# A slot table of 128 partition rows, and source lanes stored as bytes, in a fused graph network

## The reference

```python
h = relu(layernorm(x))
for W, b in lift:                                 # 8 times
    g = l2_normalize(segment_sum(h[src] * edge_weight[:, None], dst))
    h = l2_normalize(concatenate([h, g]) @ W + b)
for W, b in proj:                                 # 4 times
    g = segment_sum(h[src] * edge_weight[:, None], dst)
    h = tanh(concatenate([h, g]) @ W + b)
x = x + h
```

## Time and profile before

| | |
|---|---|
| median of 3 runs | 12909.68 us |
| profiled execution | 12883.4 us, its span 12881.8 us |
| busy in the span: PE, DVE, ACT, POOL | 7922.8, 9363.2, 3162.7, 4996.6 us |
| mean DMA rate | 94 GB/s |
| granted clock of TensorE, mean | 0.765 |

### The profile page before, as it was taken

How to read it: one execution, slowest core, us unless ns; L and a number is a source line. 1 busy time by engine, 2 the same in 40 slices (tenths; PEclk the granted TensorE clock), 3 DMA queues, 4 the chain that set the end, 5 groups by cost and what they waited for, 6 DMA issues and landing times.

```text
span 12881.8 us, 342702 instructions
## 1 busy us (share of the span) xinstructions
PE 7922.8 (62%) x130026; PEld 5298.1 (41%) x130039; DVE 9363.2 (73%) x19419; ACT 3162.7 (25%) x7975; POOL 4996.6 (39%) x5027
## 2 busy tenths in 40 slices
PE   2444444410376777776776777777667777777773
PEld 1333333300365666665665666666522222222221
DVE  7666666637665675666666666666699999999995
ACT  0000000008421212212211212212134444444431
POOL 2666666620112112111111111111077777777771
PEclk9999999995678787787787787787755565555555
DMA  4000000017645454454454454454422212222221
GB/s 152 21 21 21 21 20 21 21 69 285 203 136 149 134 153 136 132 168 120 132 166 119 135 161 132 139 161 135 116 43 36 35 35 35 35 35 35 35 34 17
DMA packets 717799, 1210.29 MB, mean 94 GB/s; under 512 B 176136, under 2 KB 338731, under 8 KB 713491
## 3 DMA queue, kind: packets, MB, share of 16 engines
q1 hardware_dynamic: 433940, 1057.96, 25.5%
q0 software_dynamic: 146832, 68.64, 5.9%
q10 hardware_dynamic: 136012, 67.95, 2.1%
HBM read 1051.25 MB, written 140.48 MB: 93 GB/s over the span
## 4 chain that ended last, share of the span: by engine, by line
PE 29%; DVE 21%; issue 16%; another core or an unknown queue 7%; DMA 3%; POOL 2%; DVEq 1%; ACT 1%; SPq 0%; POOLq 0%; ACTq 0%
PE psum L1927 10%; PE psum L1959 8%; PE psum L1942 6%; DVE space L1439 3%; DVE space L1472 2%; DVE space L1473 2%; PE psum L2034 2%; DMA space<-src_rows 2%; DVE space L1435 2%; DVE space L1407 1%; PE psum L2004 1%; DVE space L1417 1%; DVE space L1484 1%; DVE space L1477 1%
## 5 line engine op out<-in xcount | busy, mean ns | idle before, releaser
L787 POOL DMA_INDIRECT space<-feature_table,space x2000 | 2422.1, 1211 | 615.2 <-issue 614.9
L714 POOL TENSOR_TENSOR claim_out<-claim_in 128x1 f32<-128x1 f32 x443 | 94.8, 214 | 6431.4 <-DMA table<-space 2772.0
L1138 DVE TENSOR_TENSOR space<-psum,space 128x320 f32<-128x320 f32 x2400 | 1065.8, 485 | 1769.1 <-PE psum L1942 1740.1
L1622 ACT ACTIVATE space<-psum 128x375 f32<-128x375 f32 x2400 | 952.4, 435 | 3886.4 <-PE psum L1927 2877.6
L2050 PE MATMUL psum<-w_mix,space 64*128 64x448 f32 x4144 | 1842.3, 986 | 0.0
L1959 PE MATMUL psum<-space 128*128 128x96 bf16 x24000 | 1472.1, 214 | 472.3 <-issue 410.8
L723 POOL DMA_INDIRECT slots<-space x1568 | 1510.5, 963 | 449.3 <-issue 413.8
L1927 PE MATMUL psum<-space 128*32 128x125 fp8e4 x72000 | 1483.7, 230 | 310.0 <-issue 304.1
L1959 PEld LDWEIGHTS psum<-space 128*128 128x128 fp8e4 x24000 | 1199.3, 101 | 716.8 <-issue 608.4
L1927 PEld LDWEIGHTS psum<-space 128*32 128x32 bf16 x72000 | 1165.2, 101 | 619.7 <-issue 613.1
L1942 PE MATMUL psum<-identity,space 128*128 128x128 f32 x6000 | 964.7, 296 | 359.5 <-ACT space L1622 346.6
(11 more groups left out here) (278 smaller groups left out, 12198.9 us busy)
## 6 DMA issues: line engine op xcount, KB each, us to landing
space<-marks SPq DMA_DIRECT2D x2400, 320.0 KB
space<-src_rows SPq DMA_DIRECT2D x102, 640.0 KB, 4.7
marks<-space SPq DMA_DIRECT2D x100, 640.0 KB, 3.1
space<-distances ACTq DMA_DIRECT2D x200, 320.0 KB
space<-block_ids SPq DMA_DIRECT2D x198, 200.0 KB
slots<-space SPq DMA_DIRECT2D x82, 448.0 KB, 9.2
space<-feature_table,space POOLq DMA_INDIRECT x2072
slots<-space POOLq DMA_INDIRECT x1608, 2.1
```

The lines of the kernel that those rows point to most:

```text
L787: g.indirect_dma_start(out=gathered_rows[0:SLOTS, half, t, :], out_offset=None, in_=feature_table, in_offset=bass.IndirectOffsetOnAxis(ap= ...
L1138: v.tensor_tensor(row[:, half, :], slots_of_unit[:, half, :], slot_w[:, bass.ds(at * UNIT_TILES + k * HALF_TILES, HALF_TILES)].rearrange(" ...
L1622: a.activation(to[:, s0:s1, :, :], pair_picked[:, bank, 0:(s1 - s0) * PICK_COLS].rearrange("p (k c r) -> p k c r", k=s1 - s0, r=CAP), ACT.Copy
```

## The change

The table's first dimension becomes 128 (`LANES`) instead of 125 (`SLOTS`). The three new rows are never scattered to and hold the empty records of the fill. The loads of the pieces and of the records, and DVE's copies, take all 128 partitions. The list and the spill records move back by 6000 records, and the number of fills stays 82 (663,696 records before and 669,696 now, in steps of 8192). POOL still gathers 125 rows per tile, and the steps from slot to slot in the scattered addresses are unchanged.

The source lanes are stored as bytes (U8): in the turned copy, in `src_rows` and in the ring that is compared. The value for "no lane" becomes 200 instead of -1, since a byte can't be negative. On every engine the instructions and their order stay the same.

```diff
@@ constants
+    U8 = mybir.dt.uint8
-    LIST_ROW = SLOTS * SLOT_TILES
+    LIST_ROW = LANES * SLOT_TILES
+    NO_LANE = 200.0
@@ tensors
-    src_rows = nc.dram_tensor("src_rows", [SRC_CHUNKS * LANES, LANES], BF16).ap()
+    src_rows = nc.dram_tensor("src_rows", [SRC_CHUNKS * LANES, LANES], U8).ap()
-    slot_tiles = slots[0:LIST_ROW, :].rearrange("(p t) w -> p t w", p=SLOTS)
+    slot_tiles = slots[0:LIST_ROW, :].rearrange("(p t) w -> p t w", p=LANES)
-        source_ring = ring_flat[:, 0:UNIT_COLS].bitcast(BF16).rearrange("p (s c) -> p s c", s=2)
+        source_ring = ring_flat[:, 0:UNIT_COLS // 2].bitcast(U8).rearrange("p (s c) -> p s c", s=2)
-        src_turned = carve(SRC_CHUNKS * LANES // 2).bitcast(BF16)
+        src_turned = carve(SRC_CHUNKS * LANES // 4).bitcast(U8)
@@ SP
-                sp.dma_start(pieces[0:SLOTS, k % 2, :, :], slot_tiles[:, k * PIECE:(k + 1) * PIECE, :]
+                sp.dma_start(pieces[:, k % 2, :, :], slot_tiles[:, k * PIECE:(k + 1) * PIECE, :]
-                sp.dma_start(rec[0:SLOTS, half, :, :], slot_tiles[:, bass.ds((2 * i + half) * UNIT_TILES, UNIT_TILES), :]
+                sp.dma_start(rec[:, half, :, :], slot_tiles[:, bass.ds((2 * i + half) * UNIT_TILES, UNIT_TILES), :]
@@ DVE
-            for at, value in ((slice(0, 1), 0.0), (slice(1, 2), -1.0), (slice(2, 3), 0.0), (slice(3, 4), -1.0),
+            for at, value in ((slice(0, 1), 0.0), (slice(1, 2), -1.0), (slice(2, 3), 0.0), (slice(3, 4), NO_LANE),
-            step(v.memset(slot_src, -1.0))
+            step(v.memset(slot_src, NO_LANE))
-                v.tensor_copy(slot_lane[0:SLOTS, at], pieces[0:SLOTS, k % 2, :, 1])
-                v.tensor_copy(slot_w[0:SLOTS, at], pieces[0:SLOTS, k % 2, :, 2])
-                v.tensor_copy(slot_row[0:SLOTS, at], pieces.bitcast(I32)[0:SLOTS, k % 2, :, 0])
-                v.tensor_copy(slot_src[0:SLOTS, at], pieces[0:SLOTS, k % 2, :, 3]).then_inc(slots_read, 1)
+                v.tensor_copy(slot_lane[:, at], pieces[:, k % 2, :, 1])
+                v.tensor_copy(slot_w[:, at], pieces[:, k % 2, :, 2])
+                v.tensor_copy(slot_row[:, at], pieces.bitcast(I32)[:, k % 2, :, 0])
+                v.tensor_copy(slot_src[:, at], pieces[:, k % 2, :, 3]).then_inc(slots_read, 1)
```

## The result

The changed kernel takes 12817.5 us in the median of five runs (12765.8 to 12841.3) against 12919.6 of the kernel before (five runs with those made beside it, 12894.7 to 12932.6): a ratio of 0.9919, 95% interval 0.9893 to 0.9944; the two medians lie 102 us apart. The profiled execution took 12817.5 us, its span 12815.9, 65.9 us less than the span in the earlier trace rows. On a second chip the same pair came to 0.993 (0.9911 to 0.9948).

What follows compares the result with a forecast made beforehand. Bounds: table loads on 5 of 16 DMA engines, and in the marks the loop of store, lane load and compare. Gains 50 + 41 + 0.5 = 91.5 us from 12909.7 gave 12818 us, range 12778 to 12872.

Steps and rivals of the forecast that it cites:

- Step 1: Table loads: 128 rows use all 16 DMA engines instead of 5, pieces 4.2 us apart instead of 10.4; gain 50 us.
- the limit by two buffers: Table loads: copies, issue, fixed time and transfer make 8.3 us per two pieces, 4.2 us each.
- Rival (c): Table loads: their rate has another cause, long steps between rows; only the marks gain, 12869 us; chance 0.05.
- Pieces 0 and 1: First two table loads, issued beside the list's work; claimed to bring nothing.
- Step 2: Marks: the lanes' load carries 320 KB instead of 640, 0.9 us less to landing; gain 41 us.
- the clean turn: Marks' loop of store, load and compare without disturbance: 8.92 us per pair of units, against 9.23 over the stage.
- rival (a): Marks: the lanes' landing is set by requests and round trips, not bytes; only the table gains, 12860 us; chance 0.13.
- Step 3: Marks: the compare (L1092) reads bytes at the same 1549 ns as bf16; 0 us.
- (b): Marks: the byte compare falls to one element per step, 2.92 us, +27 us; 12887 us in all; chance 0.07.
- (d): Marks: the compare reads bytes at half the slow rate, 5.84 us; kernel slower, 13179 us; chance 0.04.
- Steps 4 and 5: Stores of src_rows halve in bytes, 0.5 us off; last network's 100 record loads go to 128 rows, 0 us.
- Within 15 us: Profile after: layers stay at 6012 us and the last network at 3527 within 15 us, else the sum is wrong.

Runs made afterwards that it cites:

- The quarter load: Changed kernel, but the lanes' load brings only 5 of a unit's 20 tiles (80 KB instead of 320); span 12785.2 us, marks 423.8 us.

## Why the prediction was right, and where it was not

The forecast was 12818 us and the median 12817.5. That close a hit is chance: five runs spread over 76 us. What can be compared is the sum of the stages, 91.5 us forecast, 87 and 92 measured. Even this agreement is in part luck: the list gave 6 us that were not in the sum, and the lanes 6 to 13 us less than their term. The steps:

- **Step 1, the table, 50 us: 52.3 and 50.1.** Right in cause (127 rows, one engine's share) and in size. The pieces came 4.0 us apart in the first profile and 4.3 to 4.4 in the seven others with 128 rows, around the 4.2 of the limit by two buffers. Rival (c) is out: 127 rows have the same long steps as 128.
- **"Pieces 0 and 1 are loaded beside the list's work before 2775.95 and bring nothing": wrong by 6 us.** They were hidden for DVE, but they slowed the work that hid them. The row was there to see: the list's second turn began 29.3 us after the first and the others 23 us after one another.
- **Step 2, the lanes, 41 us: 27.9, and 34.9 on the second chip.** Right in cause, but this term was mis-sized. I had taken 0.9 us per turn, the bytes at the rate of the busy engines; the median landing fell by 0.4 to 0.5 us (4.7 to 4.3 or 4.2). The turn can be added up from the starts in the two timelines, as means over the units 4 to 97: store issue to load issue, load issue to DVE's start, DVE's start to the next store. Before it is 0.61 + 5.01 + 3.61 = 9.23 us, now 0.60 + 4.47 + 3.61 = 8.68 us. So the whole gain, 0.54 us per turn, is in the landing (0.70 on the second chip, 5.09 to 4.39), and nothing else in the turn moved. The sum also shows where the 0.31 us above the clean turn sat: mostly in landings that come later than in that one turn (a mean of 5.01 us to DVE's start where it has 4.77); what delays them was not looked for. Of the miss of 0.27 us per turn, 0.36 is too much gain taken (0.9 for 0.54), and about 0.1 comes back because I had added 0.4 for disturbance where 0.3 stayed. The quarter load fits: about 4.1 us of landing are there with a quarter of the bytes. So half of rival (a) was true. My own low end, half of the 0.9 us and 22 us of gain, was the nearer reading on the first chip, the forecast on the second.
- **Step 3, the compare, 0: right**, 1549 ns for bytes. Rivals (b) and (d) are out.
- **Steps 4 and 5, -0.5 and 0: right** within what shows: turning took 0.6 us less, the last network 1.3 us less.
- **The end effects.** The sort took 20 us more and the layers 2 us more in that one profile; neither was in the sum. "Within 15 us" for layers was right by luck; 43 us between profiles of unchanged layers is what chip B shows.

The range, 12778 to 12872, held the median. The side forecast with 0.86, faster by more than 0.3%, came true: the interval 0.9893 to 0.9944 lies wholly beyond it.

## What to carry to other kernels

Read the DMA share of a load that something waits for: a share that stays at a small n/16 (0.31 and 0.06 here) says that the split over the engines, not the memory, is the limit; then change the first dimension, as 125 to 128 here, even if that moves more bytes. Before cutting bytes, halve them once more in an experiment that leaves work out, since a landing time that doesn't follow is hidden by issuing earlier, into more buffers, and not by shrinking. And when two transfers share one queue, the one whose landing closes the tightest loop goes first: here the same four buffers gave 452 us in one order and 388 in the other, and with two buffers it was 455 and 426 to 429.

## What the runs showed of the hardware

- The rate of a load goes by its number of rows so sharply that 127 rows were 11 times slower than 128 (428.8 against 36 to 38 us). The Trainium skill, "DMA: Bandwidth & Descriptors", section "Why a DMA increments its semaphore by 16 and not by 1", says that a DMA uses the largest number of engines up to 16 that divides the slowest dimension on both of its sides, and 1 for 127 partitions. The trace agrees: shares of 0.06, 0.31 and 0.88 for 127, 125 and 128 rows. For 126 rows, by that rule 14 engines, it shows 0.75, below 14/16.
- A load on few engines slows what other queues move beside it: a turn of the list takes 29.3 to 29.5 us beside pieces of 125 rows, 28.8 to 29.4 beside 127 rows, and 23 us alone or beside pieces of 128 rows.
- One kernel took 12.8 to 12.9 ms on some chips and 11.3 to 11.4 ms on others, with the stages bound by DMA and DVE equal to some us. The durations of instructions are equal too (the sort's L932 980 ns and L1869 285 ns on both); what differs is waits. It is not the granted clock: in the sort it is 1.00 in both profiles of the kernel before, and in the changed kernel's on chip B it is 0.50 with the sort as short. On the slow chip DVE waited 116.4 us in 400 us of the sort (400 to 800 us) for something that the profile calls remote, and on the fast one none of that shows. The row of the slow chip:

```profile
DVE space L981 <- remote: 116.4, 33, 4.3
```

L981 waits for two small matrix products that by the profile had ended some 4 us before (609.4 us, and DVE starts at 613.18). This points at PE's signal coming late, but no run shows it, and what on the chip delays it was not found.
